# Other places in the engines' orders for routing's slots, a delayed projection and a late sum, in a fused attention and mixture-of-experts layer

## The chip, the cores and the metric

The kernel runs as one launch on one core of a Trainium2 chip. The metric is the device time of the launch in microseconds (us). Five engines work side by side, each through its own list of instructions, in order: TensorE (PE), VectorE (DVE), ScalarE (ACT), GpSimd (POOL) and SyncE (SP, which only issues DMAs). They meet only at semaphores. ACT and POOL issue DMAs too.

## The reference

2,048 tokens (32 sequences of 64) of width 256 go through cross attention and a feed-forward layer, both gated and with a residual. In short:

```python
n = layernorm(x)
q, k_new, v_new = n @ wq.T, n @ wk.T, n @ wv.T
k = concat([ctx, k_new]); v = concat([ctx, v_new])        # per sequence of 64
x = x + tanh(g_xattn) * (softmax(q @ k.T / 16) @ v) @ wo.T
n = layernorm(x)
probs = softmax(n @ gate_w.T)                              # 8 experts
top_p, top_i = top_k(probs, 2)
y = sum over the 2 chosen experts of top_p * (silu(n @ fc1.T) * (n @ fc2.T)) @ proj.T   # width 176
shared = (silu(n @ s1.T) * (n @ s2.T)) @ sproj.T           # width 704
x = x + tanh(g_ffn) * (y + sigmoid(n @ gate_s.T) * shared)
```

## The kernel before, in words

The tokens are worked on in 4 chunks of 512 (4 tiles of 128 rows). Every matrix product is made of three: each operand is split into a rounded part ("hi", written by ACT as it copies a result out of PSUM) and the rest ("lo", PSUM minus hi, by DVE, or POOL for the context and some weights), and PE adds hi·hi, hi·lo and lo·hi. So a result of PE that another product reads takes the way PE, ACT, DVE, PE.

**The start.** PE first runs empty transposes (`warm`, on the identity that comes with the constants). SP loads x of chunk 0 in two halves, the attention weights `wa` in three pieces, the context of chunk 0 (`CR`) and x of chunk 1. The context of chunk 1 goes into the same buffer, so its load waits until ACT (`cached_hi`) and POOL (`cached_lo`) have read the first one; constants for routing and x of chunk 2 are queued on SP behind it. On POOL `rstd1(1)`, which gives the layer-norm factors of chunk 1, stands behind `cached_lo(0)`; on ACT the copy of the product of the v and o weights (`WVO`), without which no `values` can start, stands behind `first_apply(1, ...)`, which needs those factors.

**A chunk of attention**, c = 0 to 3, tiles j = 0 to 3: `scores(c, j)`, `row_max` (DVE) and `exps` (ACT), `probs_t` (transposes of the probabilities), `values(c, j)` (the value rows times WVO), `attend(c, j)` (probabilities times values), and on DVE `residual(c, j)` and `aggregate`. In between lie the projections of the next chunk, `project(c + 1, i)`, i = 0 to 3, which share one PSUM bank: each waits until `project_lo` of the one before has read it; `scores(c + 1, 0)` waits for the fourth. Also in between: the norms of the chunk before and its routing.

**Routing of chunk c - 2** during chunk c: `two_best` and `counts` on DVE; `route` (PE, two small fp32 products that count rows before each row); `slots` (DVE, seven small steps, each waiting for the one before) gives each token's places. `scatter(c, i)` on POOL then writes the rows to DRAM, sorted by expert, by 4 indirect DMAs each.

**The rest.** The shared layer of chunks 0 to 2 runs in blocks j = 0 to 5: `fc` (up products), `s_silu` (ACT), `s_mult` (DVE), `s_hi` (ACT), `s_lo` (DVE), `pj` (projection into four PSUM banks that gather all six blocks). Then come 39 expert tiles, each about 2 us of PE, and at last the shared layer of chunk 3, in which block 4 is the short one (64 rows) and block 5 a full one. In that stage the expert results come back from DRAM (`y2_d`, by 8 DMAs of 512 KB), are added in eight `combine(n)`, four on DVE (0, 2, 4, 7) and four on POOL (1, 3, 5, 6), and stored; chunk 3 gets its shared part added in `s_last(t)`.

The order is written out by hand, one list for each engine. These lines of it matter most, DVE's in a chunk (lines 1397 to 1420) and PE's wait in `attend`:

```python
row_max(c, 2)
residual(c, 0)
if c > 1:
    slots(c - 2)
v_lo(c, 1)
second_lo(c - 1, 1)
probs_lo(c, 1)
project_lo(c + 1, 1)
row_max(c, 3)
residual(c, 1)
aggregate(c, 0)
```

`attend(c, 1)` waits in this order: for `slots(c - 2)` (v_pos), with its second product for `v_lo(c, 1)` (v_v), with its third for `probs_lo(c, 1)` (v_pt).

## Time and profile before

| | us |
|---|---|
| median of 3 runs (294.42 to 295.42) | 294.89 |
| the profiled execution, its own time | 294.28 |
| its span, first to last instruction | 292.5 |
| PE busy | 272.9 |
| DVE busy | 213.9 |
| ACT busy | 170.7 |
| POOL busy | 136.1 |
| mean granted TensorE clock, as a share of full | 0.999 |

The profiled execution lies 0.61 us below the median of the runs. The profile gives the busy time of each engine, the waits with what ended them, and a timeline. "Busy" of PE is modelled at the ends of products; the start of an instruction is the sharper number. A wait is put down to what came last.

### The profile page before, as it was taken

To read this page: it belongs to the slowest core of one execution; us is meant where nothing else is said; L and a number is where in the kernel's file an instruction comes from. 1 tells how busy PE (TensorE), PEld (TensorE's weight loads), DVE (VectorE), ACT (ScalarE), POOL (GpSimd) and SP (SyncE) were. 2 spreads that over 40 slices of the span, in tenths; PEclk is the share of its full clock that TensorE was granted. 3 is DMA by queue.
4 is the path that set the end of the run, shared out by engine and by line. 5 is a ranking of instruction groups with operands and counts; after the bars stand their busy time and mean duration, and the time that the engine had idled before them with its cause. 6 is when DMAs were issued, how large, how long until landed. Compare 5 with 4: busy or idle time off the path is not lost.

```text
span 292.5 us, 5859 instructions
## 1 busy us (share of the span) xinstructions
PE 272.9 (93%) x1777; PEld 245.7 (84%) x1777; DVE 213.9 (73%) x694; ACT 170.7 (58%) x401; POOL 136.1 (47%) x161
## 2 busy tenths in 40 slices
PE   3998899999899899999999999899999999999992
PEld 3887789789778677888788888899999999998882
DVE  6867776979869759768776767868778777763285
ACT  2775678687566567473335446566666667654240
POOL 2420831441784427453450000068778778776141
PEclk9999999999999999999999999999999999999999
DMA  6470244221136112544425744368888888756796
GB/s 194 190 256 2 73 149 141 72 80 50 38 91 242 74 40 85 186 144 125 150 76 182 247 140 145 131 113 134 136 141 134 136 139 137 116 69 72 291 354 217
DMA packets 25022, 40.18 MB, mean 137 GB/s; under 512 B 2976, under 2 KB 18976, under 8 KB 24992
## 3 DMA queue, kind: packets, MB, share of 16 engines
q1 hardware_dynamic: 16272, 27.43, 29.1%
q0 software_dynamic: 7152, 9.57, 19.4%
q10 hardware_dynamic: 1568, 2.80, 2.7%
q8 instruction: 15, 0.25, 0.4%
q14 instruction: 15, 0.12, 0.2%
HBM read 22.68 MB, written 17.11 MB: 136 GB/s over the span
## 4 chain that ended last, share of the span: by engine, by line
PE 57%; DVE 23%; issue 7%; ACT 6%; DMA 3%; POOL 1%; SPq 0%; DVEq 0%; ACTq 0%; POOLq 0%
PE bank L437 43%; PE bank L702 8%; DVE ew_lo L1097 4%; DMA xn_all<-x_dram 3%; PE bank L801 3%; PE bank L755 3%; DVE work L1453 2%; ACT ew_hi L830 2%; DVE xt_lo L1097 2%; ACT sh_hi L830 2%; DVE neg_max L1145 2%; DVE sh_lo L1097 2%; DVE ln_stats L1108 1%; DVE work L1168 1%; ACT work L862 1%
## 5 line engine op out<-in xcount | busy, mean ns | idle before, releaser
L1650 POOL DMA_INDIRECT y_d<-work,dest_of_slot x39 | 60.5, 1552 | 56.2 <-DVE dest_of_slot L1504 54.7
L437 PE MATMUL bank<-ew_hi,xt_hi 128*128 (+2 forms) x172 | 53.9, 323 | 1.4 <-DVE xt_lo L1097 0.7
L437 PE MATMUL bank<-ew_lo,xt_hi 128*128 (+2 forms) x172 | 51.7, 301 | 0.0
L437 PE MATMUL bank<-ew_hi,xt_lo 128*128 (+1 forms) x133 | 40.5, 305 | 0.0
L1610 POOL DMA_INDIRECT xs_d<-xn_all,slot_of_pair x32 | 33.3, 1042 | 10.1 <-issue 7.3
L1097 DVE TENSOR_TENSOR xt_lo<-bank,xt_hi 128x256 fp32r<-128x256 f32 (+2 forms) x90 | 35.5, 397 | 3.2 <-ACT xt_hi L830 2.0
L437 PE MATMUL bank<-xt_hi,sw_hi 128*128 128x512 f32 x88 | 34.8, 395 | 0.2 <-DVE work L1453 0.2
L437 PE MATMUL bank<-xt_lo,sw_hi 128*128 128x512 f32 x88 | 34.5, 392 | 0.0
L437 PE MATMUL bank<-xt_hi,sw_lo 128*128 128x512 f32 x88 | 34.3, 390 | 0.0
L830 ACT ACTIVATE xt_hi<-bank 128x256 fp32r<-128x256 f32 (+1 forms) x90 | 32.7, 409 | 2.4 <-PE bank L801 1.1
L437 PEld LDWEIGHTS bank<-ew_hi,xt_hi 128*128 128x128 f32 (+1 forms) x172 | 32.4, 189 | 2.0 <-DVE xt_lo L1097 0.9
L437 PE MATMUL bank<-ew_hi 128*128 128x256 f32 (+1 forms) x100 | 30.8, 314 | 3.4 <-DVE ew_lo L1097 2.0
L437 PEld LDWEIGHTS bank<-ew_lo,xt_hi 128*128 128x128 f32 (+1 forms) x172 | 32.7, 190 | 0.1
L1097 DVE TENSOR_TENSOR ew_lo<-bank,ew_hi 128x512 fp32r<-128x512 f32 (+1 forms) x41 | 22.6, 580 | 13.2 <-ACT ew_hi L830 13.1
L830 ACT ACTIVATE sh_hi<-work 128x512 fp32r<-128x512 f32 (+1 forms) x24 | 15.2, 632 | 28.8 <-DVE work L1453 25.2
L437 PE MATMUL bank<-ew_hi,ew_lo 128*128 128x256 f32 (+1 forms) x100 | 30.4, 310 | 1.5 <-DVE ew_lo L1097 1.5
L437 PE MATMUL bank<-ew_lo,ew_hi 128*128 128x256 f32 (+1 forms) x100 | 29.7, 304 | 0.6 <-DVE ew_lo L1097 0.2
L702 PE MATMUL bank<-sw_hi,sh_hi 128*128 128x256 f32 x96 | 27.2, 289 | 0.3 <-DVE work L1468 0.2
L830 ACT ACTIVATE ew_hi<-bank 128x512 fp32r<-128x512 f32 (+1 forms) x45 | 21.6, 518 | 9.3 <-PE bank L437 8.2
L702 PE MATMUL bank<-sw_lo,sh_hi 128*128 128x256 f32 x96 | 26.6, 282 | 0.0
L437 PEld LDWEIGHTS bank<-ew_hi,xt_lo 128*128 128x128 f32 x133 | 25.1, 188 | 0.0
L1490 DVE TENSOR_TENSOR work<-work,bank 128x176 f32<-128x176 f32 x39 | 13.1, 337 | 16.0 <-ACT work L1025 16.0
(161 smaller groups left out, 678.8 us busy)
## 6 DMA issues: line engine op xcount, KB each, us to landing
work<-xs_d SPq DMA_DIRECT2D x39, 136.0 KB, 2.5
weight_stage<-ew_dram SPq DMA_DIRECT2D x10, 486.5 KB, 3.7
y_d<-work SPq DMA_DIRECT2D x6, 512.0 KB, 3.9
work<-ctx_t_dram SPq DMA_DIRECT2D x4, 512.0 KB, 3.3
ew_hi<-y_d SPq DMA_DIRECT2D x4, 512.0 KB, 8.1
ew_hi<-y_d ACTq DMA_DIRECT2D x4, 512.0 KB, 7.0
xn_all<-x_dram SPq DMA_DIRECT2D x3, 512.0 KB, 6.6
xs_d<-pad_row SPq DMA_DIRECT2D x9, 136.0 KB, 2.0
```

The lines of the kernel that those rows point to most:

```text
L437: last = nc.tensor.matmul(dst, a, b, start=(n == 0), stop=(n == len(pairs) - 1))
L702: last = nc.tensor.matmul(B[4 + t][:, 0:D], h[:, t * P:(t + 1) * P], w, start=(j == 0 and n == 0), stop=(j == S_FULL and n == len(parts) - 1))
L755: last = nc.tensor.transpose(rows_bank(n)[:, k * P:(k + 1) * P], EX[:, w, k * P:(k + 1) * P], ident)
L801: last = nc.tensor.transpose(B[4 + v][:, i * P:(i + 1) * P], EH[:, v, i * P:(i + 1) * P], ident)
L830: return nc.scalar.activation(dst, src, ACT.Copy, scale=scale)
L862: nc.scalar.activation(XA[:, j, :], XNR[:, c * TPC + j, :], ACT.Identity, bias=nb1[:, j:j + 1], scale=rs1[:, j:j + 1]).then_inc(a_xn, 1)
L1097: return nc.vector.tensor_tensor(dst, src, hi.bitcast(F32), ALU.subtract)
L1145: last = nc.vector.tensor_reduce(nmx[r, j % 2:j % 2 + 1], own_keys(B[4 + j % 2], b), mybir.AxisListType.XY, ALU.max, negate=True)
L1453: nc.vector.tensor_tensor(SHF[0:rows, j % 2, :], STH[0:rows, j % 2, :], h2, ALU.mult).then_inc(v_h, 1)
L1490: nc.vector.tensor_tensor(EH[:, u % 2, 0:F_E], ETH[:, u % 2, :], B[2 + u % 2][:, F_E:2 * F_E], ALU.mult)
L1610: nc.gpsimd.indirect_dma_start(out=xs_d, out_offset=bass.IndirectOffsetOnAxis(ap=POS[:, i, n:n + 1], axis=0), in_=XN[:, n, :], in_offset=N ...
L1650: nc.gpsimd.indirect_dma_start(out=y2_d, out_offset=bass.IndirectOffsetOnAxis(ap=IX[:, n:n + 1], axis=0), in_=EY[:, n % 4, :], in_offset=None,
```

## The change

It moves work within the lists; no product of the computation is added or left out.

- **Start.** SP issues x of chunk 1 ahead of the context of chunk 0. ACT issues the constants' DMA ahead of the gates'. `warm` is 13 and 3 products, 16 in place of 18, and none stand between the two halves of `first_norm(0)`. DVE does `weight_lo(2)` and `(3)` ahead of `project_lo(0, 0)`, `ln1_stats(2)` behind `row_max(0, 2)` and `project_lo(1, 0)` ahead of `residual(0, 0)`. In chunk 1 PE does `scores(1, 0)` between the halves of `first_norm(2)`.
- **Slots.** `route(c - 2)` goes behind `attend(c, 1)`, into bank B[4] for chunks 0 and 1, and `slots(c - 2)` behind `aggregate(c, 0)`. `attend(c, 1)` loses its wait for v_pos; `scores(3, 0)` gets one for `slots(0)`. POOL's scatters move behind `rstd2`.
- **Chunk 2.** `attend(2, 2)` goes behind `project(3, 3)`, `residual(2, 2)` behind `project_lo(3, 3)`.
- **The last chunk's shared layer.** PE does fc 1, pj 0, fc 2, fc 3, pj 1, fc 4, fc 5, pj 2 to pj 5, where it did fc 1, pj 0, fc 2, pj 1, fc 3, pj 2, fc 4, fc 5, pj 3 to pj 5. ACT does `s_silu` of block 5 ahead of `s_hi` of block 4, DVE `s_mult` of block 5 ahead of `s_lo` of block 4, and `combine(7)` ahead of the four `s_last`. POOL's `combine(6)` waits until `s_lo` of the last block is done (v_hl).

The core of the diff:

```diff
@@ block.sync
+            load_x(1)
             sp.dma_start(CR, ctx_t[0]).then_inc(d_ct, 16)
-            load_x(1)
@@ scores
+                    if c > 2:
+                        waits += [(0, v_pos, c - 2)]
@@ attend
-                if j == 1 and c > 1:
-                    waits = waits + [(0, v_pos, c - 1)]
@@ route
-                bank, o = (B[1], 0) if c == LAST else (B[7], D)
+                bank, o = (B[1], 0) if c == LAST else (B[7], D) if c == LAST - 1 else (B[4], 0)
...
+                elif c == LAST - 1:
+                    pe.wait_ge(v_x2, 4 * (c + 2))
                 else:
-                    pe.wait_ge(v_x2, 4 * (c + 2))
+                    pe.wait_ge(a_exp, 4 * (c + 2) + 3)
@@ block.tensor, start
-            warm(10)
+            warm(13)
             first_norm(0, 0)
-            warm(4)
             first_norm(0, 1)
-            warm(4)
+            warm(3)
@@ block.tensor, chunks
-                if 0 < c < LAST:
+                if c == 1:
                     first_norm(c + 1, 0)
+                    scores(c, 0)
                     first_norm(c + 1, 1)
...
                 values(c, 1)
-                if c > 1:
-                    route(c - 2)
...
                 attend(c, 1)
+                if c > 1:
+                    route(c - 2)
...
-                attend(c, 2)
+                if c != LAST - 1:
+                    attend(c, 2)
                 values(c, 3)
                 probs_t(c, 3)
                 if c < LAST:
                     project(c + 1, 3)
-                else:
+                if c == LAST - 1:
+                    attend(c, 2)
+                if c == LAST:
@@ block.tensor, end
             fc(LAST, 1)
+            pj(LAST, 0)
+            fc(LAST, 2)
+            fc(LAST, 3)
+            pj(LAST, 1)
+            fc(LAST, 4)
+            fc(LAST, 5)
             for j in range(2, S_BLK):
-                if j < S_FULL:
-                    pj(LAST, j - 2)
-                fc(LAST, j)
-            for j in range(S_FULL - 2, S_BLK):
                 pj(LAST, j)
@@ block.scalar
-            act.dma_start(C[:], consts).then_inc(d_const, 16)
...
-                s_silu(LAST, j)
+                if j < S_FULL:
+                    s_silu(LAST, j)
+                if j == S_FULL - 1:
+                    s_silu(LAST, S_FULL)
                 s_hi(LAST, j)
@@ block.vector, end
-                s_mult(LAST, j)
-                if j in (3, 5):
-                    combine((0, 4)[j // 5])
+                if j < S_FULL:
+                    s_mult(LAST, j)
+                if j == 3:
+                    combine(0)
+                if j == S_FULL - 1:
+                    s_mult(LAST, S_FULL)
+                if j == S_FULL:
+                    combine(4)
                 s_lo(LAST, j)
                 if j == 3:
                     combine(2)
+            combine(7)
             for t in range(TPC):
                 s_last(t)
-            combine(7)
@@ block.gpsimd
+                if c == LAST:
+                    scatter(c - 3, 1)
+                rstd2(c, 0)
                 if c > 1:
                     scatter(c - 2, 0)
-                rstd2(c, 0)
...
-                if 1 < c < LAST:
-                    scatter(c - 2, 1)
...
             for n in (1, 3, 5, 6):
+                if n == 6:
+                    pool.wait_ge(v_hl, 6 * N_CH)
                 combine(n)
```

What this does to three lists (semaphores in brackets). **SP at the start**, before:

```order
L315 DMA xn_all<-x_dram 128x2x256 x2
L319 DMA weight_stage<-wa_dram 128x512 x2
L319 DMA weight_stage<-wa_dram 128x1024
L320 DMA work<-ctx_t_dram 128x1024
L304 DMA xn_all<-x_dram 128x4x256
L312 DMA work<-ctx_t_dram 128x1024 [waits g_ct,a_ct]
L323 DMA work<-rconsts_dram 128x823
L304 DMA xn_all<-x_dram 128x4x256
```

and now:

```order
L315 DMA xn_all<-x_dram 128x2x256 x2
L319 DMA weight_stage<-wa_dram 128x512 x2
L319 DMA weight_stage<-wa_dram 128x1024
L304 DMA xn_all<-x_dram 128x4x256
L321 DMA work<-ctx_t_dram 128x1024
L312 DMA work<-ctx_t_dram 128x1024 [waits g_ct,a_ct]
L323 DMA work<-rconsts_dram 128x823
L304 DMA xn_all<-x_dram 128x4x256
```

Row 4 and 5 have changed places: x of chunk 1 is queued ahead of the context of chunk 0.

**DVE in chunk 2**, from `residual(2, 0)` (work from bank, scale and xn_all) on, with the slots as the rows that wait for p_route and v_route, and `v_lo` the row that waits for a_v. Before, with equal steps left out:

```order
L1168 SCALAR_TENSOR_TENSOR work<-bank,softmax_scale,xn_all 128x256 [waits a_xn2,p_av,d_x2,v_rd]
L1172 BN_STATS ln_stats<-work 128x6 [waits v_x2]
L1259 TENSOR_TENSOR work<-work,bank 128x32 [waits p_route]
L1262 SCALAR_TENSOR_TENSOR slot_of_pair<-work 128x2x4 [waits v_route]
L1264 COPY work<-work 128x8 [waits v_route]
L1097 TENSOR_TENSOR ew_lo<-bank,ew_hi 128x512 [waits a_v]
L1097 TENSOR_TENSOR xt_lo<-bank,xt_hi 128x2x256 [waits a_x2t]
L1097 TENSOR_TENSOR ew_lo<-bank,ew_hi 128x256 [waits a_pt]
L1135 SCALAR_TENSOR_TENSOR sh_lo<-bank,sh_hi 128x512 [waits a_qk]
L1145 TENSOR_REDUCE neg_max<-bank 64x1 [waits p_sc]
L1168 SCALAR_TENSOR_TENSOR work<-bank,softmax_scale,xn_all 128x256 [waits p_av]
L1178 BN_AGGR ln_mean_var<-ln_stats 128x2 [waits g_rs2,v_st2]
```

and now:

```order
L1183 SCALAR_TENSOR_TENSOR work<-bank,softmax_scale,xn_all 128x256 [waits a_xn2,p_av,d_x2,v_rd]
L1187 BN_STATS ln_stats<-work 128x6 [waits v_x2]
L1112 TENSOR_TENSOR ew_lo<-bank,ew_hi 128x512 [waits a_v]
L1112 TENSOR_TENSOR xt_lo<-bank,xt_hi 128x2x256 [waits a_x2t]
L1112 TENSOR_TENSOR ew_lo<-bank,ew_hi 128x256 [waits a_pt]
L1150 SCALAR_TENSOR_TENSOR sh_lo<-bank,sh_hi 128x512 [waits a_qk]
L1160 TENSOR_REDUCE neg_max<-bank 64x1 [waits p_sc]
L1183 SCALAR_TENSOR_TENSOR work<-bank,softmax_scale,xn_all 128x256 [waits p_av]
L1193 BN_AGGR ln_mean_var<-ln_stats 128x2 [waits g_rs2,v_st2]
L1274 TENSOR_TENSOR work<-work,bank 128x32 [waits p_route]
L1279 COPY work<-work 128x8 [waits v_route]
L1112 TENSOR_TENSOR ew_lo<-bank,ew_hi 128x512 [waits a_v]
```

The slots now stand behind the second `residual` and `aggregate`; `v_lo`, `second_lo`, `probs_lo`, `project_lo` and `row_max` have moved ahead of them.

**DVE at the end**: `s_mult` (work from work and bank), `s_lo` (sh_lo or sh_hi), `combine` (xn_all from ew_hi) and `s_last` (waits p_end). Before:

```order
L1097 TENSOR_TENSOR sh_lo<-work,sh_hi 128x512 [waits a_hh]
L1453 TENSOR_TENSOR work<-work,bank 64x512 [waits v_hl,a_th]
L1097 TENSOR_TENSOR sh_hi<-work,sh_hi 64x512 [waits a_hh]
L1453 TENSOR_TENSOR work<-work,bank 128x512 [waits v_hl,a_th]
L1440 TENSOR_TENSOR xn_all<-ew_hi 128x2x256 [waits d_y1_1,d_y0_1]
L1097 TENSOR_TENSOR sh_lo<-work,sh_hi 128x512 [waits a_hh]
L1483 SCALAR_TENSOR_TENSOR xn_all<-bank,shared_gate,xn_all 128x256 [waits p_end,v_c2]
L1483 SCALAR_TENSOR_TENSOR xn_all<-bank,shared_gate,xn_all 128x256 [waits p_end]
L1483 SCALAR_TENSOR_TENSOR xn_all<-bank,shared_gate,xn_all 128x256 [waits p_end,g_c2]
L1440 TENSOR_TENSOR xn_all<-ew_hi 128x2x256 [waits d_y1_2,d_y0_2]
```

and now:

```order
L1112 TENSOR_TENSOR sh_lo<-work,sh_hi 128x512 [waits a_hh]
L1471 TENSOR_TENSOR work<-work,bank 64x512 [waits v_hl,a_th]
L1471 TENSOR_TENSOR work<-work,bank 128x512 [waits v_hl,a_th]
L1112 TENSOR_TENSOR sh_hi<-work,sh_hi 64x512 [waits a_hh]
L1458 TENSOR_TENSOR xn_all<-ew_hi 128x2x256 [waits d_y1_1,d_y0_1]
L1112 TENSOR_TENSOR sh_lo<-work,sh_hi 128x512 [waits a_hh]
L1458 TENSOR_TENSOR xn_all<-ew_hi 128x2x256 [waits d_y1_2,d_y0_2]
L1501 SCALAR_TENSOR_TENSOR xn_all<-bank,shared_gate,xn_all 128x256 [waits p_end,v_c2]
L1501 SCALAR_TENSOR_TENSOR xn_all<-bank,shared_gate,xn_all 128x256 [waits p_end]
L1501 SCALAR_TENSOR_TENSOR xn_all<-bank,shared_gate,xn_all 128x256 [waits p_end,g_c2]
```

The last `combine`, for chunk 2's results (d_y1_2, d_y0_2), now runs ahead of the four `s_last`, and `s_mult` of the last block ahead of `s_lo` of the short one.

## Rows read from the trace of the kernel before

**Rows 1.** The page, busy time of each engine.
```profile
PE 272.9 (93%) x1777; PEld 245.7 (84%) x1777; DVE 213.9 (73%) x694; ACT 170.7 (58%) x401; POOL 136.1 (47%) x161
```

**Rows 2.** Waits of PE: us in total, times, longest.
```profile
PE bank L437 <- DVE ew_lo L1097: 3.7, 7, 1.5
PE bank L437 <- DVE sh_lo L1135: 0.9, 1, 0.9
```

**Rows 3.** Timeline, PE, the start: start, length, engine, line, operation, idle before.
```profile
4.22 2.39 PE L592 MATMUL bank<-consts_sb 128*128 128x128 f32 x10 [4.22 <-DMA consts_sb<-consts_dram]
8.98 0.60 PE L592 MATMUL bank<-consts_sb 128*128 128x128 f32 x4
9.83 0.73 PE L437 MATMUL bank<-ew_hi 128*128 128x512 f32 x2 [0.25 <-ACT ew_hi L830]
...
24.46 0.38 PE L437 MATMUL bank<-ew_hi 128*128 128x256 f32 x1 [1.45 <-DVE ew_lo L1097]
```

**Rows 4.** Timeline, all engines, from the first context load to the third x load.
```profile
10.33 1.06 ACT L830 ACTIVATE ew_hi<-work 128x1024 fp32r<-128x1024 f32 x1
11.47 2.83 POOL L1596 TENSOR_TENSOR ew_lo<-work,ew_hi 128x256 fp32r<-128x256 f32 x4 [4.48 <-ACT ew_hi L830]
11.67 1.41 DVE L1108 BATCH_NORM_STATS2 ln_stats<-xn_all 128x6 f32<-128x256 f32 x4 [0.57 <-DMA xn_all<-x_dram]
16.97 1.09 ACT L862 ACTIVATE work<-xn_all,ln_bias,ln_rstd 128x256 f32<-128x256 f32 x2 [0.67 <-POOL ln_bias L1570]
21.86 1.41 DVE L1108 BATCH_NORM_STATS2 ln_stats<-xn_all 128x6 f32<-128x256 f32 x4 [1.48 <-DMA xn_all<-x_dram]
```

**Rows 5.** Timeline, DVE, chunk 0.
```profile
28.04 1.02 DVE L1097 TENSOR_TENSOR ew_lo<-bank,ew_hi 128x512 fp32r<-128x512 f32 x2 [1.61 <-ACT ew_hi L830]
33.08 0.69 DVE L1135 SCALAR_TENSOR_TENSOR sh_lo<-bank,sh_hi 128x512 fp32r<-128x512 f32 x1 [0.62 <-ACT sh_hi L830]
```

**Rows 6.** Timeline, chunk 2 around the slots of chunk 0.
```profile
72.64 0.30 PE L580 MATMUL bank<-work 128*128 128x32 f32 x2
73.00 0.63 PE L445 MATMUL bank<-consts_sb,xn_all 128*128 128x128 f32 x4
...
74.10 0.60 ACT L830 ACTIVATE ew_hi<-bank 128x512 fp32r<-128x512 f32 x1
74.22 0.17 DVE L1259 TENSOR_TENSOR work<-work,bank 128x32 f32<-128x32 f32 x1
75.76 0.68 DVE L1097 TENSOR_TENSOR ew_lo<-bank,ew_hi 128x512 fp32r<-128x512 f32 x1
...
77.43 0.39 PE L437 MATMUL bank<-ew_hi,ew_lo 128*128 128x256 f32 x1 [0.55 <-DVE ew_lo L1097]
```

**Rows 7.** Timeline, DVE, from chunk 2 to chunk 3.
```profile
87.09 0.69 DVE L1097 TENSOR_TENSOR sw_lo<-bank,sw_hi 128x512 fp32r<-128x512 f32 x1 [0.59 <-ACT sw_hi L830]
88.87 1.31 DVE L1145 TENSOR_REDUCE neg_max<-bank 64x1 f32<-64x128 f32 x4
```

**Rows 8.** Timeline, PE, second value product of chunk 3.
```profile
99.32 0.38 PE L437 MATMUL bank<-ew_hi,ew_lo 128*128 128x256 f32 x1 [0.55 <-DVE ew_lo L1097]
```

**Rows 9.** Timeline, the end.
```profile
285.10 1.27 POOL L1660 TENSOR_TENSOR xn_all<-ew_hi 128x512 f32<-128x512 f32 x1 [2.28 <-DMA ew_hi<-y_d]
...
285.19 1.72 DVE L1097 TENSOR_TENSOR sh_lo<-work,sh_hi 128x512 fp32r<-128x512 f32 x1
287.47 1.66 DVE L1483 SCALAR_TENSOR_TENSOR xn_all<-bank,shared_gate,xn_all 128x256 f32<-128x256 f32 x4 [0.56 <-PE bank L702]
289.05 0.68 DVE L1440 TENSOR_TENSOR xn_all<-ew_hi 128x512 f32<-128x512 f32 x1
...
289.76 0.39 ACTq L1090 DMA_DIRECT2D out_dram<-xn_all  x1
```

**Rows 10.** The page, DMA issues: engine, count, size, median us to landing.
```profile
out_dram<-xn_all ACTq DMA_DIRECT2D x1, 256.0 KB, 2.1
```

**Rows 11.** Windows: PE, PEld, DVE, ACT, POOL busy (instructions), granted clock, DMA share.
```profile
9.80:15.50 5.70, 5.67 (x25) 4.62 (x25) 5.08 (x14) 4.28 (x7) 4.03 (x6) 1.00 0.22 75
```

More of the change, by code:

```diff
@@ L641, in _ @@
             for c in range(1, N_CH):
-                if 0 < c < LAST:
+                if c == 1:
                     first_norm(c + 1, 0)
+                    scores(c, 0)
                     first_norm(c + 1, 1)
-                scores(c, 0)
-                scores(c, 1)
+                    scores(c, 1)
+                else:
+                    if c < LAST:
+                        first_norm(c + 1, 0)
+                        first_norm(c + 1, 1)
+                    scores(c, 0)
+                    scores(c, 1)
                 values(c, 0)
@@ L830, in copy @@
                 return nc.scalar.activation(dst, src, ACT.Copy, scale=scale)
+            act.dma_start(C[:], consts).then_inc(d_const, 16)
             act.dma_start(G[:], gates).then_inc(tanh_g, 16)
-            act.dma_start(C[:], consts).then_inc(d_const, 16)
             act.dma_start(RWF[:], rw).then_inc(d_rw, 16)
@@ L1249, in slots @@
                 dve.wait_ge(p_r, c + 1)
-                at = B[7][:, D:D + NB].rearrange("p (e t) -> p e t", e=N_E)
+                at = (B[7][:, D:D + NB] if c == LAST - 1 else B[4][:, 0:NB]).rearrange("p (e t) -> p e t", e=N_E)
                 if c == LAST:
@@ L1339, in _ @@
             ln1_stats(1)
-            project_lo(0, 0)
             weight_lo(2)
             weight_lo(3)
+            project_lo(0, 0)
             project_lo(0, 1)
@@ L1355, in _ @@
             row_max(0, 1)
-            ln1_stats(2)
             v_lo(0, 0)
@@ L1361, in _ @@
             row_max(0, 2)
+            ln1_stats(2)
             v_lo(0, 1)
             probs_lo(0, 1)
+            project_lo(1, 0)
             residual(0, 0)
-            project_lo(1, 0)
             row_max(0, 3)
@@ L1398, in _ @@
                 residual(c, 0)
-                if c > 1:
-                    slots(c - 2)
                 v_lo(c, 1)
@@ L1411, in _ @@
                     ln1_stats(c + 2)
+                if c > 1:
+                    slots(c - 2)
                 v_lo(c, 2)
@@ L1418, in _ @@
                     project_lo(c + 1, 2)
-                residual(c, 2)
+                if c != LAST - 1:
+                    residual(c, 2)
                 v_lo(c, 3)
@@ L1423, in _ @@
                     project_lo(c + 1, 3)
+                if c == LAST - 1:
+                    residual(c, 2)
                 residual(c, 3)
```

## The prediction

> **What bounds the kernel now.** I read the busy times first: PE is busy for 93% of the span and DVE for 73% [rows 1]. So most of what DVE, ACT and POOL do costs nothing, and only stretches in which PE stands still can be won. The waits of PE say which: 3.7 us in seven for copies at line 1097 and 0.9 us in one for `project_lo` [rows 2], besides the first 4.22 us, for the constants [rows 3]. The timeline then gives each its place: 1.45 us before the product at 24.46 [rows 3], 0.55 us before 77.43 and again before 99.32 [rows 6, 8], and a last stretch in which PE is through and DVE, POOL and the stores finish [rows 9]. The reader should see that DVE is the engine behind all of them. What PE gains in one place it keeps only until the next copy that DVE owes it.
>
> The sum is made against the profiled execution: 294.28 us, of which 292.5 is the span and 1.8 lies around it. The median of the runs is 0.61 higher. About 0.3%, 0.88 us, is what a measurement can tell from no change.
>
> **The start: +0.1 us.** The constants' DMA is first on ACT. The engine issues a DMA in about 0.4 us (row at 289.76 [rows 9]), so PE's first product comes some 0.4 earlier than 4.22. Two of 18 empty products go (0.21 to 0.24 each at the start, 2.39 us for ten [rows 3]). Both only bring PE sooner to its first real product, at 9.83, which waits for an ACT copy [rows 3]: I cost them at nothing. That ACT copy hides them; without it they would be worth at most 0.6.
>
> The swap of the two loads is the real edit. The load of x of chunk 1 is the last of the first group: DVE starts on it at 11.67, after waiting for its DMA, 1.34 later than ACT starts `cached_hi(0)` on the context at 10.33 [rows 4]. Both are 512 KB, so I take it that the two arrivals change places. Then `cached_hi(0)` starts at about 11.7, `cached_lo(0)`, which waits for it, at 12.8 in place of 11.47, and behind it on POOL the factors of chunk 1. ACT's `first_apply(1)` waits for these at 16.97 [rows 4] and goes to 18.3, the WVO copy behind it too, and `values(0, 0)` with it: a loss of up to 1.3. Against it stands the 1.45 stall at 24.46 [rows 3]. It comes from DVE's `ln1_stats(2)`, which waited for its load until 21.86 with the value copies queued behind it (1.48 idle, then 1.41 of work [rows 4]). With that step moved behind `row_max(0, 2)` the stall goes. So the one late chain takes the other's place, and the product at 24.46 stays about there: 0.
>
> The moved `ln1_stats(2)`, 1.41 and its short steps, some 1.8 in all, falls into the 1.61 us that DVE is idle before 28.04 [rows 5], which leaves 0.2. `project_lo(1, 0)` ahead of `residual(0, 0)` removes the 0.9 wait [rows 2], but the next projection needs the `project_lo` at 33.08, which waited for ACT [rows 5], whose `exps` hang on the same DVE steps. I take +0.1 for the three. `scores(1, 0)` between the norm's halves fills PE, but its transposes still wait for ACT: 0. The two `weight_lo` that come earlier now lie beside POOL's context copies instead of its norm steps: 0. Ends for the whole start: -1.4 (the swap costs nothing and the stall goes) to +0.6 (the two chains add in part, a third of the 1.34, plus 0.2).
>
> **Slots and chunk 2: -0.75 us.** `slots(0)` keeps DVE from 74.22 to 75.76, where `v_lo(2, 1)` starts; ACT had its half ready at 74.10 + 0.60 = 74.70 [rows 6]. Without the slots `v_lo` and the three copies behind it come 75.76 - 74.72 = 1.04 earlier. The third product of `attend(2, 1)` goes from 77.43 to 76.39. The 0.55 before it [rows 6] is then gone, and the rest of 1.04 comes from the first two, which waited for v_pos. `route(0)`, 73.00 - 72.64 = 0.36 of PE [rows 6], was hidden ahead of this stall and is now behind it: 1.04 - 0.36 = **-0.68** there. `slots(0)` itself now ends some 3 us later. What needs it: POOL's scatters, which nobody awaits in attention, and `scores(3, 0)`, shortly ahead of the 88.87 of [rows 7] and some 10 us later; both are covered.
>
> `attend(2, 2)` behind `project(3, 3)`: its six products (0.39 for one of the long shape [rows 6], less for the rest; I take 1.2 with their waits) leave the path of `project_lo(3, 3)`, which goes from 87.09 to about 85.9. But `residual(2, 2)` comes behind it on DVE, about 1.0, and only then can `row_max(3, 0)` start: it stood at 88.87 [rows 7] and goes to about 88.7. Of the 1.2 only 0.15 stays. In chunk 3 the third product at 99.32, after 0.55 of wait, [rows 8] shows the same picture as chunk 2. I take 0.95 for `slots(1)`, together with the 0.15 a lead of 1.10, less 0.36 for `route(1)`: **-0.75**. The gain of chunk 2 doesn't add to that. It would have to pass `row_max(3, 0)`, which waits on DVE's queue, and I count it as used up there. From there PE has work without a break (93% [rows 1]), so the lead is carried to the end. Ends: 0 (a later DVE copy takes all) to -1.3 (chunk 2's lead is half kept).
>
> **The tail: -1.5 us.** PE's new order of `fc` and `pj` adds up to the same products, and the last block's `s_hi` is still awaited: 0. The last `s_lo`, at 285.19, took 1.72, where the same kind of instruction takes 0.68 (75.76) or 0.69 [rows 6, 7, 9]. POOL's `combine(6)` ran beside it, from 285.10 for 1.27 [rows 9]: both read two operands in SBUF, and the one excluded the other. Held back until `s_lo` is done, it lets it end 1.03 earlier, with it the last third product and `s_last(0)`: 287.47 to 286.4. `combine(7)`, 0.68 at 289.05 [rows 9], moves into DVE's wait for PE ahead of `s_last`. Its store, the last one, then no longer waits for it: the last thing to be issued is the store behind `s_last(3)`, 286.4 + 1.66 = 288.1, issued at about 288.3. The last store was issued at 289.76 [rows 9]. With 2.1 to landing [rows 10] the end is 290.4 in place of 291.9: **-1.5**. The added wait has nothing queued behind it on POOL but stores; `combine(6)` ends near 287.9 and its store lands before 290.4. Ends: -1.7, and -0.5 if POOL starts first and `combine(7)` has to stand behind its 1.27.
>
> The Trainium skill (SBUF — State Buffer, "SBUF: two separate sides") says that VectorE and GpSimd share an exclusive lock, that whoever starts first keeps it for its whole instruction, and that the other is fully blocked. By it up to the whole 1.27 could be lost at a meeting, and the tail would be -1.7 rather than -1.5. The sum goes by the 1.03 of the row, which agrees with it in kind.
>
> **Sum.** +0.1 - 0.75 - 1.5 = -2.15: 294.28 becomes 292.1 for a profiled execution, 294.89 becomes **292.7** for the median.
>
> **Rivals.**
> *The swap is free.* If the context isn't later by being queued last (its arrival is bound by something else than its place), `values(0, 0)` stays and the 1.45 stall goes: another -1.4, **291.2**. For it: the 1.45 is plain in the rows. Against: `cached_hi(0)` and DVE's start are 1.34 apart, as two loads one behind the other would be. 0.18.
> *The tail gives a third.* `combine(6)` gets in first, and `combine(7)` holds up `s_last`: -0.5 in place of -1.5, **293.7**. For it: the release by v_hl comes just when DVE itself turns to `combine(7)`. 0.13.
> *The middle gives nothing.* `residual(2, 2)` or the moved slots put another copy late: **293.4**. 0.11.
> *Both small*: **294.4**, within 0.3% of before. 0.13.
> *Slower: the clock.* The first ten empty products take 2.39 us, 0.24 each, the four at 8.98 take 0.60, 0.15 each with the last one's end [rows 3]: PE begins at 1.2 GHz and is at 2.4 before its first real product, though the granted clock reads 1.00 throughout. The new order has two empty products fewer, begins earlier, and has a longer wait before `values(0, 0)`. If the pace were not up by 9.8, the 25 instructions until 15.5, 5.67 us of busy PE [rows 11], would take twice as long: 292.7 + 5.7 = **298.4**. It decides from 2.2 us of such products on, where it has eaten the gain. Against it: PE waits 1.45 us in [rows 3], and the product behind that wait takes 0.38, as the one at 77.43 does. 0.05.
> The Trainium skill (TensorE: Matmul & The Clock Gate, Part 4) says that transposes in PE mode do not count as busy for the clock gate. By it the number of empty ones would not matter, and the first real products would run at the lower level before and after. The row at 8.98 speaks against it.
>
> **How the numbers follow.** 0.40 for the forecast, the likeliest, and 0.18, 0.13, 0.11, 0.13 and 0.05 for the rest. Faster by over 0.3%: 0.40 + 0.18 + 0.13 + 0.11 = 0.82; same 0.13; slower 0.05. The range runs from 290.6 (the free swap, with the middle's far end, -0.55) to 294.3, which leaves out the clock and most of "both small".
>
> **What would show it.** In the new profile: `cached_hi(0)` starting at about 11.7 and `values(0, 0)` about 1.3 later than before (the swap costs); at 10.3 it is the first rival. No 1.45 wait for `ln1_stats(2)`'s sake. The third products of `attend(2, 1)` and `attend(3, 1)` near 76.4 and 98.2, `row_max(3, 0)` near 88.7. The last `s_lo` 0.7 long; at 1.7 the hold did nothing. `combine(7)` ahead of `s_last`, the last store issued near 287.7, 288.3 less the 0.65 won before. A mean granted clock as before, 0.999; clearly less makes the prediction wrong, as would a new PE wait above 1 us in chunk 1 or chunk 3.

## The result, and the profile of the changed kernel

| | us |
|---|---|
| before, median of 20 runs (294.25 to 296.75) | 295.06 |
| changed, median of 20 runs (295.00 to 298.58) | 296.46 |
| ratio, with its 95% interval | 1.0045 (1.0025 to 1.0066) |
| forecast | 292.7 (290.6 to 294.3) |
| the profiled execution of the changed kernel | 298.58 |
| its span, against 292.5 before | 296.8 |

The change made the kernel slower by 1.4 us at the medians (1.3 us by the ratio), where I had forecast 2.2 us faster. The profiled execution is the longest of the 20, 2.1 us above their median, so it shows more than the median has. The page of the changed kernel, busy times [rows 1]:

```profile
PE 275.5 (93%) x1775; PEld 246.8 (83%) x1775; DVE 212.5 (72%) x694; ACT 170.6 (57%) x401; POOL 137.5 (46%) x161
```

TensorE was busy 2.6 us longer with two products fewer. Its waits (us in total, times, longest), to hold against [rows 2]:

```profile
PE bank L437 <- DVE ew_lo L1112: 3.3, 5, 1.3
PE bank L437 <- ACT ew_hi L842: 2.3, 3, 1.6
```

The copies of VectorE are waited for a little less. A new wait of 1.6 us stands at a copy of ScalarE. The start, as in [rows 4], with ScalarE's `first_apply(1)` and, last, the row of `values(0, 0)`:

```profile
12.37 1.06 ACT L842 ACTIVATE ew_hi<-work 128x1024 fp32r<-128x1024 f32 x1 [1.97 <-DMA work<-ctx_t_dram]
...
13.51 3.74 POOL L1619 TENSOR_TENSOR ew_lo<-work,ew_hi 128x256 fp32r<-128x256 f32 x4 [5.95 <-ACT ew_hi L842]
...
18.96 1.09 ACT L874 ACTIVATE work<-xn_all,ln_bias,ln_rstd 128x256 f32<-128x256 f32 x2 [2.45 <-POOL ln_bias L1593]
...
21.32 0.39 PE L437 MATMUL bank<-ew_hi 128*128 128x256 f32 x1 [1.26 <-DVE ew_lo L1112]
```

`cached_hi(0)` now waits for its DMA and starts 2.04 later than at 10.33. `cached_lo(0)` takes 3.74 in place of 2.83, but the steps of GpSimd behind it take less: from its start to that of `first_apply(1)` it is 5.45 (18.96 - 13.51), where it was 5.50 (16.97 - 11.47). `values(0, 0)` starts at 21.32, 2.0 later than before (19.32). Chunks 2 and 3, as in [rows 6 to 8]: the third product of `attend(2, 1)`, then on DVE `project_lo(3, 3)`, the two residuals and `row_max(3, 0)`, then ScalarE's last step of `exps` and its copy for `v_lo(3, 1)`, and the first and third products of `attend(3, 1)`:

```profile
76.93 0.39 PE L437 MATMUL bank<-ew_hi,ew_lo 128*128 128x256 f32 x1 [0.39 <-DVE ew_lo L1112]
...
86.54 0.69 DVE L1112 TENSOR_TENSOR sw_lo<-bank,sw_hi 128x512 fp32r<-128x512 f32 x1 [0.82 <-issue]
...
87.34 0.48 DVE L1183 SCALAR_TENSOR_TENSOR work<-bank,softmax_scale,xn_all 128x256 f32<-128x256 f32 x1
...
88.20 0.47 DVE L1183 SCALAR_TENSOR_TENSOR work<-bank,softmax_scale,xn_all 128x256 f32<-128x256 f32 x1
...
89.33 0.87 DVE L1160 TENSOR_REDUCE neg_max<-bank 64x1 f32<-64x128 f32 x3
...
96.28 0.19 ACT L903 ACTIVATION_READ_ACCUMULATOR work<-bank,neg_max 64x1 f32 x1
97.30 0.60 ACT L842 ACTIVATE ew_hi<-bank 128x512 fp32r<-128x512 f32 x1 [0.83 <-remote]
...
98.71 0.38 PE L437 MATMUL bank<-ew_hi 128*128 128x256 f32 x1 [1.59 <-ACT ew_hi L842]
...
99.60 0.39 PE L437 MATMUL bank<-ew_hi,ew_lo 128*128 128x256 f32 x1 [0.39 <-DVE ew_lo L1112]
```

ScalarE is free at 96.47 and starts the copy at 97.30, after 0.83 us that the profile puts down to "remote"; TensorE waits 1.59 for it. What follows stands in the windows (busy PE, PEld, DVE, ACT, POOL, then granted clock, DMA share, GB/s):

```profile
100.00:101.00 1.00, 1.00 (x9) 0.86 (x9) 0.63 (x3) 0.91 (x4) 0.00 (x0) 1.00 0.00 0
101.00:104.00 3.00, 3.00 (x13) 2.65 (x12) 1.82 (x10) 0.59 (x2) 1.84 (x6) 0.50 0.25 93
104.00:105.00 1.00, 1.00 (x10) 0.83 (x8) 0.00 (x0) 0.34 (x1) 0.70 (x2) 0.79 0.00 0
```

A clock of 0.79 over the last microsecond means that 0.42 of it are at half. So TensorE runs at 1.2 GHz from 101.0 to 104.4, 3.4 us. That is the drop of my slower rival, but in another place.

A second copy of ScalarE is late in this execution, the one ahead of the last `attend`, at full clock:

```profile
109.32 0.87 ACT L842 ACTIVATE ew_hi<-bank 128x512 fp32r<-128x512 f32 x2 [2.16 <-PE bank L437]
```

It starts 0.97 us after the product ahead of it (108.35), where in a0_after, a later run of the same kernel, it is 0.20 (105.84 after 105.64). So 0.77 are lost here too.

The end, as in [rows 9]: the last `s_lo`, `combine(6)`, the four `s_last`, and two of the last stores (`combine(6)`'s on SyncE, `combine(7)`'s on ScalarE):

```profile
288.21 0.69 DVE L1112 TENSOR_TENSOR sh_lo<-work,sh_hi 128x512 fp32r<-128x512 f32 x1
...
288.98 1.69 POOL L1683 TENSOR_TENSOR xn_all<-ew_hi 128x512 f32<-128x512 f32 x1 [3.23 <-DVE sh_lo L1112]
...
289.45 1.66 DVE L1501 SCALAR_TENSOR_TENSOR xn_all<-bank,shared_gate,xn_all 128x256 f32<-128x256 f32 x4
...
290.69 0.37 SPq L422 DMA_DIRECT2D out_dram<-xn_all  x1
...
291.15 0.45 ACTq L1105 DMA_DIRECT2D out_dram<-xn_all  x1
```

`s_lo` takes 0.69, as forecast. But the span ends at 296.8, 4.3 later than before, though `s_last` starts only 1.98 later than at 287.47.

### The profile page after: what moved, and what is told of

It is laid out like the page before. It is cut to its first block, busy times and chain, and to the rows that moved or that the text cites. A ratio compares the mean times of both kernels' runs of the same rounds, so it can differ in the third digit from the quotient of the medians.

```text
span 296.8 us, 5856 instructions
## 1 busy us (share of the span) xinstructions
PE 275.5 (93%) x1775; PEld 246.8 (83%) x1775; DVE 212.5 (72%) x694; ACT 170.6 (57%) x401; POOL 137.5 (46%) x161
## 4 chain that ended last, share of the span: by engine, by line
PE 55%; DVE 18%; ACT 10%; issue 10%; DMA 2%; POOL 2%; another core or an unknown queue 0%; DVEq 0%; ACTq 0%; SPq 0%; POOLq 0%
PE bank L437 41%; PE bank L712 7%; DVE ew_lo L1112 5%; ACT ew_hi L842 4%; PE bank L811 3%; PE bank L765 3%; DVE neg_max L1160 2%; ACT work L903 2%; DVE xt_lo L1112 2%; DVE ln_stats L1123 1%; DVE work L1471 1%; ACT sh_hi L842 1%; POOL ew_lo L1619 1%; DMA weight_stage<-ew_dram 1%; DMA xn_all<-x_dram 1%
## 5 line engine op out<-in xcount | busy, mean ns | idle before, releaser
L1633 POOL DMA_INDIRECT xs_d<-xn_all,slot_of_pair x32 | 34.0, 1063 | 10.2 <-issue 7.3
L437 PEld LDWEIGHTS bank<-ew_hi 128*128 128x128 f32 x100 | 18.7, 188 | 8.5 <-ACT ew_hi L842 4.1
```

Of the source, the lines that this page charges most:

```text
L437: last = nc.tensor.matmul(dst, a, b, start=(n == 0), stop=(n == len(pairs) - 1))
L1633: nc.gpsimd.indirect_dma_start(out=xs_d, out_offset=bass.IndirectOffsetOnAxis(ap=POS[:, i, n:n + 1], axis=0), in_=XN[:, n, :], in_offset=N ...
```

## Where the time went, by the trace

TensorE's lag or lead against the kernel before, at the same product in both:

| product | before | changed | difference |
|---|---|---|---|
| `attend(2, 1)`, third | 77.43 | 76.93 | -0.50 |
| `attend(3, 1)`, third | 99.32 | 99.60 | +0.28 |
| `probs_t(3, 2)` | 102.24 | 104.45 | +2.21 |
| last block's third product | 286.97 | 288.95 | +1.98 |
| end of the span | 292.5 | 296.8 | +4.3 |

Of the 1.93 between the second and the third row, 0.36 is `route(1)`, which now stands in between, and the rest is the stretch at half clock. The lag then grows to 3.1 to 3.3 in the expert tiles, 0.77 of it by the second late copy. The tail's edits took off 1.1, and then the end lost 2.3. So two things were to be explained: the halved clock, and an end that came 7.3 us after the first `s_last`, where it was 5.0.

One number stood out. GpSimd's last `combine` ended at 285.10 + 1.27 = 286.37 before and at 288.98 + 1.69 = 290.67 now. The span ended 6.1 us later both times. I made this theory A. Theory B was SyncE's queue: the stores of `s_last` stand there behind a wait for `combine(6)`.

## Experiments

**The changed kernel again** (a0_after, a1_after), without an edit.

> The changed kernel once more, as the mark for the three runs beside it: about 296.5 us at the median, 1.4 us slower than before. Theory A (the tail is bound by GpSimd's last work): the span ends 6.1 us after the end of combine(6), as it does in the profiled executions of both kernels (286.37 + 6.1 = 292.5, 290.67 + 6.1 = 296.8). Theory B (the tail is bound by the stores that stand behind combine(6) on SyncE's queue): that distance is a coincidence and will differ. The 1.6 us wait of TensorE before the second attend of chunk 3 and the 3.4 us at a granted clock of 0.5 behind it: if they belong to the order, they come again; if they are an accident of one execution, they may be missing.

> The changed kernel a third time. If the share of executions with the dip (mean clock under 0.992) is what moves its median, those without it take 294.5 to 295.8 us again, as in both measurements so far, and those with it about 1.7 to 2.5 us more; the median lies anywhere between 294.7 and 296.5. If the two measurements differ by something else, the executions without the dip will lie apart too.

Measured: 294.74 us, ratio 0.9978 (0.9959 to 0.9997), and 294.62 us, 0.9990 (0.9963 to 1.0017). Both lie below the first measurement. The first 20 runs hold ten at 295.0 to 296.1 and ten at 296.9 to 298.6, these at a mean clock of 0.983 to 0.992; in the repeats all but one, which lies far outside, took 294.3 to 295.8 us. The kernel before has both kinds in every measurement: 8 of 20, 10 of 23 and 7 of 23 runs at 295.7 us or more in these three, in the two repeats at 0.987 to 0.991. The profile of a0_after shows what is missing:

```profile
96.10 0.60 ACT L842 ACTIVATE ew_hi<-bank 128x512 fp32r<-128x512 f32 x1
...
97.51 0.38 PE L437 MATMUL bank<-ew_hi 128*128 128x256 f32 x1 [0.77 <-ACT ew_hi L842]
...
98.40 0.39 PE L437 MATMUL bank<-ew_hi,ew_lo 128*128 128x256 f32 x1 [0.39 <-DVE ew_lo L1112]
...
284.68 0.69 DVE L1112 TENSOR_TENSOR sh_lo<-work,sh_hi 128x512 fp32r<-128x512 f32 x1
...
285.45 1.68 POOL L1683 TENSOR_TENSOR xn_all<-ew_hi 128x512 f32<-128x512 f32 x1 [2.97 <-DVE sh_lo L1112]
...
core 0: 293.2 us, clock 0.997
```

The copy follows without the 0.83, TensorE waits 0.77, and no stretch at half clock follows. The third product of `attend(3, 1)` has a lead of 0.92. Against this run the first profiled execution lost 0.83 and 0.77 by the two late copies and 1.5 by the stretch. The end still comes 285.45 + 1.68 + 6.1 = 293.2. So the tail's loss is the change's own. The drop of the clock and the late copies are events of some executions.

**Holding back, undone** (t1_no_hold), on the changed kernel.

```diff
-                if n == 6:
-                    pool.wait_ge(v_hl, 6 * N_CH)
```

> GpSimd's combine(6) starts when its loads have landed, as before the change. Theory A: GpSimd ends 1.2 to 1.7 us earlier, the last s_lo takes 1.7 us again if the two meet, and the time falls by 1 to 1.7 us against the changed kernel. My prediction's own step (holding back is worth 1.03 us) says the opposite: it becomes slower by about 1 us. Theory B: SyncE's stores start earlier, the time falls by 0.7 us or less.

**`combine(6)` on VectorE** (t2_dve6).

```diff
@@ block.sync
-            sp.wait_ge(g_c2, 4)
+            sp.wait_ge(v_c2, 4)
@@ block.scalar
-            act.wait_ge(v_c2, 4)
+            act.wait_ge(v_c2, 5)
@@ block.vector, end
+            combine(6)
             combine(7)
@@ block.gpsimd
-            for n in (1, 3, 5, 6):
-                if n == 6:
-                    pool.wait_ge(v_hl, 6 * N_CH)
+            for n in (1, 3, 5):
                 combine(n)
```

> combine(6) is done by VectorE behind the last s_lo, ahead of combine(7), and GpSimd is through after combine(5). Theory A: nothing of GpSimd is left to wait for, the last s_lo takes 0.7 us, and the end is set by the last stores: 1.6 to 2.5 us faster than the changed kernel. Theory B: the stores start at the same place as in the changed kernel less the 1.7 us of combine(6) on GpSimd, 0.5 to 1 us faster.

**The store behind those of `s_last`** (t3_store_last): on SyncE the two blocks change places.

> combine(6) stays held back, but its store goes behind the stores of s_last on SyncE's queue. Theory A: no change against the changed kernel (within 0.3 us), since GpSimd ends when it did. Theory B: 0.7 us faster.

Measured, on one chip with a0_after's 294.74: 293.56, 292.78 and 294.68 us. Undoing the hold makes the changed kernel 1.2 us faster, where my prediction's step says 1 us slower. Rows of the three, each with its span last (t1_no_hold, t2_dve6, t3_store_last):

```profile
284.18 0.69 DVE L1112 TENSOR_TENSOR sh_lo<-work,sh_hi 128x512 fp32r<-128x512 f32 x1
...
284.37 1.65 POOL L1683 TENSOR_TENSOR xn_all<-ew_hi 128x512 f32<-128x512 f32 x1 [2.42 <-DMA ew_hi<-y_d]
...
284.79 1.78 DVE L1458 TENSOR_TENSOR xn_all<-ew_hi 128x512 f32<-128x512 f32 x1
...
core 0: 292.1 us, clock 0.997
```

```profile
280.81 1.29 POOL L1684 TENSOR_TENSOR xn_all<-ew_hi 128x512 f32<-128x512 f32 x1 [0.77 <-DMA ew_hi<-y_d]
...
285.17 1.29 DVE L1458 TENSOR_TENSOR xn_all<-ew_hi 128x512 f32<-128x512 f32 x2
...
288.05 0.46 ACTq L1105 DMA_DIRECT2D out_dram<-xn_all  x1
...
core 0: 291.0 us, clock 0.997
```

```profile
284.94 1.68 POOL L1683 TENSOR_TENSOR xn_all<-ew_hi 128x512 f32<-128x512 f32 x1 [2.81 <-DVE sh_lo L1112]
...
286.32 1.13 SPq L422 DMA_DIRECT2D out_dram<-xn_all  x2
287.49 0.45 SPq L425 DMA_DIRECT2D out_dram<-xn_all  x1
...
core 0: 292.7 us, clock 0.996
```

In t1_no_hold GpSimd ends at 286.02 and the span 6.1 later; the meeting is now with `combine(7)`, which takes 1.78, and `s_lo` keeps its 0.69. In t3_store_last the stores have changed places, the time hasn't changed, and 286.62 + 6.1 = 292.7: theory B falls. In t2_dve6 GpSimd ends at 282.10, which binds nothing, and the span ends 2.9 us after the issue of the last store at 288.05. The 1.96 us under a0_after are most of what the end had lost. In the raw records each engine's list ends with an instruction called DRAIN and some semaphore events. GpSimd's DRAIN ends 5.9 us after its last `combine`, in t2_dve6 as elsewhere. In a0_after it is the last of the five to end, 0.23 us before the span, and SyncE's, which follows the wait for all stores, ended 1.65 us earlier. In t2_dve6 SyncE's is the last and GpSimd's ends 2.8 us before it. In the kernel before they were level: SyncE's ended 0.14 us before GpSimd's.

**The hold alone on the kernel before** (t4_before_hold).

> The kernel before with one edit: GpSimd's combine(6) waits for the last s_lo. Theory A (the span ends 6.1 us after GpSimd's last work): s_lo takes 0.7 us and TensorE's last products come 1.0 us earlier, but GpSimd ends at about 287.2 to 287.6 instead of 286.37, so the whole becomes 0.8 to 1.3 us slower. My prediction's step: 1.0 us faster, since nothing waits for GpSimd. Rival B (stores on SyncE's queue): within 0.3 us.

Measured: 296.11 us, ratio 1.0042 (1.0019 to 1.0065).

```profile
286.55 0.39 PE L702 MATMUL bank<-sw_hi,sh_lo 128*128 128x256 f32 x1 [0.22 <-DVE sh_lo L1097]
...
286.58 1.30 POOL L1660 TENSOR_TENSOR xn_all<-ew_hi 128x512 f32<-128x512 f32 x1 [3.14 <-DVE sh_lo L1097]
...
core 0: 294.0 us, clock 0.994
```

The last block's third product comes at 286.55 instead of 286.97, though TensorE was 0.6 to 0.7 later in the expert tiles. GpSimd ends at 287.88, and 287.88 + 6.1 = 294.0. One line of the change alone makes the kernel before 1.2 us slower.

**`combine(6)` on VectorE in the kernel before** (w1_before_dve6).

> The kernel before with one edit: combine(6) on VectorE behind the last s_lo, ahead of s_last. GpSimd ends with combine(5), whose end plus 6.1 us lies before the last store, and s_lo takes 0.7 instead of 1.7 us: 0.9 to 1.3 us faster than before. If GpSimd's end had not been a bound, the gain were only the 1.03 of s_lo less what combine(6) holds up s_last, 0.6 to 0.9.

Measured: a median of 294.41 us, in which two of the 12 runs lie far outside (334 and 380 us). Without them it is 293.70, ratio 0.9960 (0.9927 to 0.9993), with a profiled span of 291.7 in place of 292.5. That is 1.2 us faster, the size that theory A expects, but the interval, 0.2 to 2.2 us, takes in the smaller size too.

**Parts of the change undone**, each on t2_dve6 (292.78 us): the loads in the old order (u1_no_swap), route, slots and scatters in their old places (u2_slots_back), `attend(2, 2)` and `residual(2, 2)` in theirs (u3_chunk2_back).

```diff
-            load_x(1)
             sp.dma_start(CR, ctx_t[0]).then_inc(d_ct, 16)
+            load_x(1)
```

> The version with combine(6) on VectorE (292.8 us), with the two loads in their old order: context of chunk 0, then x of chunk 1. If the swap only moves a late chain from one load to the other (my prediction's 0), the time stays within 0.4 us, with values(0, 0) 1.3 us earlier and the copies behind ln1_stats(1) later. If the swap costs (rival: values(0, 0) is the only late one, since ln1_stats(2) has been moved anyway), it becomes 0.6 to 1.4 us faster.

> The same version with route, slots and the scatters in their old places. My prediction's step says that moving them was worth 0.75 us: 0.6 to 0.9 us slower than 292.8. Rival (the queue of VectorE takes it back): within 0.3 us.

> The same version with attend(2, 2) and residual(2, 2) in their old places. In the changed kernel row_max(3, 0) starts at 89.0 to 89.3 instead of 88.87 although TensorE was 0.9 us ahead at 87: the move costs what residual(2, 2) takes. Theory: undoing it keeps the lead, 0.3 to 0.8 us faster. My prediction had 0.15 for the move: 0.15 slower, not measurable.

Measured: 291.63, 294.87 and 292.47 us. These three ran on another chip than t2_dve6, one on which the kernel before took 294.91 in place of 295.36, so differences to t2_dve6 can be off by half a microsecond. The swap costs 1.15 by these medians and 0.6 by the ratios to the kernel before. Between two versions on the same chip that differ in it alone, u3_chunk2_back and v1_best below, it costs 1.22. In u1_no_swap the context is there earlier and x of chunk 1 later:

```profile
11.01 1.06 ACT L842 ACTIVATE ew_hi<-work 128x1024 fp32r<-128x1024 f32 x1 [0.85 <-DMA work<-ctx_t_dram]
...
12.15 3.30 POOL L1620 TENSOR_TENSOR ew_lo<-work,ew_hi 128x256 fp32r<-128x256 f32 x4 [4.63 <-ACT ew_hi L842]
...
12.36 1.40 DVE L1123 BATCH_NORM_STATS2 ln_stats<-xn_all 128x6 f32<-128x256 f32 x4 [1.40 <-DMA xn_all<-x_dram]
...
23.69 0.39 PE L437 MATMUL bank<-ew_hi 128*128 128x256 f32 x1
```

The product at 24.46 [rows 3] stands at 23.69, against 24.36 in t2_dve6 and 24.72 in a0_after. The late x of chunk 1 costs nothing. u2_slots_back has runs of both kinds (293.5 to 295.7), so its profile is the better measure of the order itself: a span of 291.9 against 291.0, and 0.93 of TensorE's lead lost at the last block (286.24 against 285.31). Its median is 2.1 above t2_dve6's, which has no run of the longer kind. u3_chunk2_back starts `row_max(3, 0)` at once behind one residual:

```profile
86.30 0.69 DVE L1109 TENSOR_TENSOR sw_lo<-bank,sw_hi 128x512 fp32r<-128x512 f32 x1 [0.58 <-ACT sw_hi L839]
86.91 0.48 DVE L1180 SCALAR_TENSOR_TENSOR work<-bank,softmax_scale,xn_all 128x256 f32<-128x256 f32 x1
...
88.08 1.31 DVE L1157 TENSOR_REDUCE neg_max<-bank 64x1 f32<-64x128 f32 x4
```

88.08 against 88.65 in t2_dve6, with equal starts. In the time it is 0.3 across the two chips, and 0.38 between u1_no_swap and v1_best on one chip, at the edge of what the runs tell apart; in the profiles' spans it is 0.7 (291.0 against 290.3).

**TensorE's old order in the tail** (v2_pe_tail_back), on v1_best below.

> The best version so far (291.25 us) with TensorE's order of fc and pj in the last chunk as before the change. My prediction costs that order at nothing: within 0.3 us of 291.25. Rival: without fc 3 and fc 5 done early, s_mult and s_hi of the last blocks come late and TensorE waits for them: 0.5 us slower or more.

Measured: 292.11 us, 0.86 slower than v1_best, which ran on another chip; by the ratios to the kernel before (0.9895 against 0.9873) it is 0.65. The wait ahead of the last block, v1_best first, then v2_pe_tail_back:

```profile
282.58 0.36 PE L709 MATMUL bank<-sw_hi,sh_hi 128*128 128x256 f32 x1 [0.16 <-DVE sh_hi L1109]
```

```profile
284.32 0.36 PE L709 MATMUL bank<-sw_hi,sh_hi 128*128 128x256 f32 x1 [0.79 <-ACT sh_hi L837]
```

With `s_mult` and `s_silu` of block 5 drawn ahead, TensorE has to follow, or it waits 0.79 for `s_hi`, 0.63 more.

**Does a wait bring the drop of the clock?** d1_pause and d2_pause put copies that nothing uses ahead of `v_hi(3, 1)` on ScalarE (three and six, each behind the one before).

```diff
                 exps(c, 2)
+                if c == LAST:
+                    for i in range(3):
+                        copy(PAUSE[:], C[:, 0:200]).then_inc(paused, 1)
+                        act.wait_ge(paused, i + 1)
                 v_hi(c, 1)
```

> The version with combine(6) on VectorE, with three idle copies of 200 columns on ScalarE ahead of v_hi(3, 1): no result uses them, they only delay it, by about 1 us, as the unexplained 0.83 us in the profiled execution of the changed kernel did. Theory (a long wait of TensorE makes its clock fall): the wait ahead of the second attend of chunk 3 grows from 0.8 to some 1.8 us, a stretch at a granted clock of 0.5 follows in most executions, and the time grows by 2.5 to 3 us. Rival (the dip comes on its own): the time grows by 1 us and no more, with the clock as before, 0.997.

> The same with six such copies, 2 us of delay. Theory: the dip in every execution, the time 3.5 to 4.5 us longer than the version without a pause. Rival: 2 us longer.

Measured: 296.09 and 297.38 us, 3.3 and 4.6 over t2_dve6 (by the ratios 3.5 and 5.1). Of the 12 runs of d1_pause one lies far outside, one took 293.87 at a clock of 1.000, and ten took 294.8 to 296.5 at 0.986 to 0.992. Its profile:

```profile
99.10 0.39 PE L438 MATMUL bank<-ew_hi 128*128 128x256 f32 x1 [1.99 <-ACT ew_hi L843]
...
101.00:104.00 3.00, 3.00 (x12) 0.50 0.26 91
```

The wait is 1.99, and 3.4 us at half clock follow (here the middle of it). They cost 1.55: TensorE's lag against t2_dve6 grows from 1.88 at `attend(3, 1)` to 3.43 at the next product that waits (105.99 against 102.56). In d2_pause the wait is 3.18 and the stretch, again 3.4 us, costs 1.5; 8 of its 10 runs are at 0.985 to 0.991, two at 0.994, where I had expected the drop in every one. In most executions, then, a wait of this length brings the drop. The Trainium skill (TensorE: Matmul & The Clock Gate, "HAM oscillation — how this bites in real kernels") says that idle gaps of TensorE, in its example long waits for DMAs, throw the engine back to the lower clock; waits of 2.0 and 3.2 us do so in these rows. But the wait isn't all of it: v2_pe_tail_back's profiled execution has such a stretch, from 97.8 to 101.2, behind waits of 0.73 and 0.55, and v1_best, with 0.78 and 0.54 in the same places, has none.

**The kernel before, once more** (b0_before).

> The kernel before, profiled once more: either 294.3 to 295.1 us at a mean clock of 0.994 to 0.999, or, if it falls among the executions at 0.987 to 0.991, about 296.3 us with a stretch at a clock of 0.5 whose place shows which wait it follows.

Measured: 294.32 us at 0.994, span 292.5. It wasn't one of the longer kind, so the place of its drop remains unseen. The 0.994 is a drop from 289.2 on, behind TensorE's last product, where it costs nothing.

**Both costly edits undone** (v1_best): t2_dve6 with the loads in the old order and chunk 2 in the old places.

> The version with combine(6) on VectorE, with both edits undone that cost: the loads in the old order (1.15 us in the run without the swap) and attend(2, 2) and residual(2, 2) in the old places (0.3 us). If the two add up: 292.8 - 1.15 - 0.3 = 291.3 us, 1.2% faster than before. If VectorE's queue eats the second: 291.6.

Measured: 291.25 us (290.73 to 292.69), ratio 0.9873 (0.9832 to 0.9915). The median comes where the two gains, added, put it. It is the fastest kernel here.

## Why the prediction was wrong

The step that failed is in the tail: "The added wait has nothing queued behind it on POOL but stores". The stores stand on SyncE, and that matters little (t3_store_last). What stood behind `combine(6)` was the end of the program on GpSimd, 6.1 us of it. The same rows that I used showed it, 285.10 + 1.27 [rows 9] against a span of 292.5, but I followed only the last store, whose landing gave nearly the same end, 291.9. Both paths were level in the kernel before (0.14 us apart by the raw records), and I pushed one of them back. Two more edits show the size: t1_no_hold gives back 1.2 us, and t4_before_hold loses 1.2 by the hold alone.

Term by term, in a0_after's profile, which has no stretch at half clock:

| term | forecast | measured | from |
|---|---|---|---|
| start | +0.1 | +0.2 | lag at 44.75 (44.91) |
| slots and chunk 2 | -0.75 | -0.7 | lead of 0.56 at 99.90 (99.34) |
| `s_lo` in the tail | -1.03 | -1.0 | 286.97 to 285.43, of which 0.5 was lead |
| rest of the tail | -0.47 | +2.2 | span 293.2 against 292.5 |
| sum | -2.15 | +0.7 | |

The sum compares two single executions, one 0.6 below the median of its runs and one 0.3 above. By the medians of the repeats the changed kernel is 0.6 and 0.4 us faster, and there a third of the runs of the kernel before are of the longer kind. The term that failed doesn't hang on this: it is read within each trace, as 6.1 us behind GpSimd's last work. (One rival's sum has a slip: without the 0.75 of the middle it is 293.5, not 293.4.)

- **Start.** Its size was right. `cached_hi(0)` was forecast at about 11.7 and came at 12.37, 12.04 and 11.59 (changed, a0_after, t2_dve6). Even with the old order of the loads it comes at 11.01, not at 10.33, so a part of its lateness isn't the swap's. I costed the two `weight_lo` beside GpSimd's context copies at 0, and that held: `cached_lo(0)` grew from 2.83 to 3.74, but the way to `first_apply(1)` didn't (5.50 and 5.45). The forecast that the swap costs was right (1.22 between u3_chunk2_back and v1_best), and so was that this loss only takes the place of the 1.45 stall.
- **Middle.** Right, by the steps forecast for the slots (76.39 came from 75.76 - 74.72; the rows give 74.70, so 0.02 more): in a0_after the third products stand at 76.57 and 98.40 for the 76.4 and 98.2 of the forecast. u2_slots_back puts the slots' move at 0.9. Chunk 2 was off: `row_max(3, 0)` came 0.07 later (88.94), not 0.15 earlier, with `project_lo(3, 3)` 0.94 ahead shortly before (86.15 against 87.09); undoing the move gains 0.3 to 0.4.
- **TensorE's order in the tail.** Costed at 0 together with that of the other engines, and together it is 0: the last `s_hi` moved from 284.52 to 284.02, by the lead. Undoing it alone costs 0.6 to 0.9, because the other engines' new orders need it.
- **The rule on the shared lock** (the Trainium skill, SBUF — State Buffer, "SBUF: two separate sides") held. Whoever met had to wait: `s_lo` 1.72 before, `combine(7)` 1.78 in t1_no_hold, and `combine(6)` 1.69 now, where it was 1.27. Holding one back moves the meeting to the next instruction with two operands in SBUF; only taking `combine(6)` off GpSimd removed it.
- **The clock.** My rival had its price and place wrong (5.7 us at the start). The start kept its clock in all profiles. The stretch came in chunk 3 and cost 1.5. In the first measurement half of the changed kernel's runs are of a longer kind, in the repeats none, so about half of the distance between 1.0045 and the forecast belongs to that kind; its one profiled execution has the two late copies beside the stretch. Why it came with the first measurement alone isn't settled; nor is what ScalarE waited for during the 0.83 and the 0.77 us. There is a sign that the slots' move keeps the drop away: runs at a clock of 0.991 or less are 14 of 34 in the edited kernels with the slots in the old place (t4_before_hold, w1_before_dve6, u2_slots_back) and none of 53 in those with both moves of the middle (a0_after, a1_after, t1 to t3, u1_no_swap). The first measurement, with 9 of 20, speaks against it, so it isn't shown.

By the repeats the change is worth 0.1 to 0.2%, hardly to be told from nothing (one interval takes in 1, the other ends at 0.9997); with the tail's fault repaired by one move (t2_dve6) it is 0.9899 (0.987 to 0.9927), 292.78 us, near the forecast, though by other terms.

## What to carry to other kernels

Before you hold an engine back near the end, follow every engine from its last instruction to the end of the span, not only the last store; the distance can be read in the profile before. Two ends that are level hide each other: shortening one gains nothing, lengthening the other costs in full. A collision is best removed by moving the work to the engine that loses by it, if that has idle time, rather than by a wait.

## What was new about the hardware

- From the end of GpSimd's last `combine` to the end of the span it took 6.1 us in eight profiles of five kernels (before and b0_before; changed, a0_after and a1_after; t1_no_hold, t3_store_last, t4_before_hold), whatever ran beside it. Of these, 5.9 us are up to the end of GpSimd's DRAIN. Where GpSimd had been done for 8.5 to 8.9 us (t2_dve6, v1_best, w1_before_dve6), the last store set the end.
- The granted clock fell to 0.5 for 3.4 us in chunk 3 behind waits of TensorE of 1.6, 2.0 and 3.2 us, and once behind 0.73 and 0.55, and each such stretch cost 1.5 to 1.6 us. Behind waits of 0.7 to 0.8 in the same place the other profiles (a0_after, t2_dve6, u2_slots_back, v1_best and the kernel before among them) have no drop in chunk 3.
